# Joining the convolution-output stage and the relation-table stage of a graph network kernel

## The reference

```python
# layer 1, its end
agg = segment_sum(m, dst)                       # 6250 x 64
h = agg @ W_lin2.T + b_lin2
out = h @ W_message_to_node.T                   # 6250 x 256
x = _layernorm(x + out, axis=-1)
# layer 2
hW = einsum('nd,rde->rne', x, weight)           # 8 tables of 6250 x 256
msg = hW[edge_type, src]
m = segment_sum(msg, dst)
x = _layernorm(x + (x @ sl_w.T + sl_b + m / deg), axis=-1)
```

## Time and profile before

| what | value |
|---|---|
| runs, median (lowest to highest) | 8941.31 us (8940.38 to 8955.18) |
| profiled execution, its time | 8943.65 us |
| profiled execution, its span | 8942.0 us |
| mean granted clock of TensorE | 0.747 of 2.4 GHz |
| first instruction of the convolution-output stage | 5191.19 us |
| first bias product of the relation stage | 5388.93 us |
| start of the last copy of the relation stage | 5869.93 us |

### The profile page before, as it was taken

One profiled execution on the slowest core, in us unless ns is written; L12 is line 12 of the kernel. 1 busy time (PEld: TensorE's weight loads), 2 busy tenths in 40 slices (PEclk: granted clock), 3 DMA queues, 4 the chain that ended last, 5 costly groups with the idle time before them and its releaser, 6 DMA issues. The chain is left out here.

```text
span 8942.0 us, 114148 instructions
## 1 busy us (share of the span) xinstructions
PE 6288.6 (70%) x23568; PEld 4316.3 (48%) x23569; DVE 4789.7 (54%) x9732; ACT 1926.0 (22%) x6808; POOL 4599.6 (51%) x4186
## 2 busy tenths in 40 slices
PE   4548899967789999676777778955555666666650
PEld 2236666635566666355666644434444443443330
DVE  4337766666566767675444431134444644444438
ACT  0223333312333333121000011100000222222221
POOL 0036666610466666004777710047777288888880
PEclk7668887777888878675555559977777788888885
DMA  1384444311444434122111123333333366666665
GB/s 38 106 216 112 112 111 111 107 46 56 149 110 112 110 108 115 36 66 62 31 31 30 31 61 133 135 107 104 104 104 104 79 68 68 68 68 68 68 68 175
DMA packets 578153, 801.90 MB, mean 90 GB/s; under 512 B 100092, under 2 KB 453709, under 8 KB 576718
## 3 DMA queue, kind: packets, MB, share of 16 engines
q0 software_dynamic: 269760, 484.09, 27.2%
q1 hardware_dynamic: 281230, 290.19, 10.8%
q10 hardware_dynamic: 27092, 26.85, 1.2%
HBM read 545.48 MB, written 255.28 MB: 90 GB/s over the span
## 5 line engine op out<-in xcount | busy, mean ns | idle before, releaser
L609 POOL DMA_INDIRECT at_x<-table,at_idx x1664 | 1626.2, 977 | 1976.2 <-ACT at_idx L726 1009.1
L2279 POOL DMA_INDIRECT acc<-sc_rows,sc_idx x832 | 1353.3, 1627 | 298.4 <-DMA acc<-sc_rows,sc_idx 185.0
L684 PE MATMUL at_psO<-at_x,at_main 128*128 128x273 f32 x3328 | 1136.7, 471 | 244.9 <-DVE agg L875 240.2
L1679 POOL DMA_INDIRECT rel_x<-rel_table,rel_idx x832 | 793.0, 953 | 963.2 <-DVE rel_sums L1760 710.0
L1679 POOL DMA_INDIRECT conv_x<-conv_table,conv_idx x832 | 808.4, 972 | 767.0 <-DVE conv_msg L1763 513.7
L684 PEld LDWEIGHTS at_psO<-at_x,at_main 128*128 128x128 f32 x3328 | 709.0, 225 | 536.3 <-issue 378.6
L1732 PE MATMUL rel_psO<-rel_x,rel_hot 128*128 128x256 f32 x1664 | 607.6, 544 | 466.6 <-DMA rel_x<-rel_table,rel_idx 394.5
L2319 PE MATMUL sc_psR<-gated,sc_pick 128*128 x1664 | 593.9, 454 | 455.0 <-ACTq L2357 451.2
L875 DVE TENSOR_TENSOR agg<-agg,at_psO 128x273 f32 x1664 | 725.4, 436 | 246.1 <-DVE agg L875 166.5
L1732 PEld LDWEIGHTS rel_psO<-rel_x,rel_hot 128*128 128x128 f32 x1664 | 463.5, 285 | 611.1 <-issue 471.6
L765 ACT COPY at_row<-at_psO 1x273 f32<-1x273 f32 x1664 | 543.0, 374 | 599.7 <-PE at_psO L684 593.5
(11 more groups left out here) (412 smaller groups left out, 9192.8 us busy)
## 6 DMA issues: line engine op xcount, KB each, us to landing
at_place<-places SPq DMA_DIRECT2D x208, 256.0 KB
rel_table<-rt_rows SPq DMA_DIRECT2D x50, 1024.0 KB
at_x<-table,at_idx POOLq DMA_INDIRECT x1664
acc<-zeros ACTq DMA_DIRECT2D x4, 6553.5 KB, 63.1
la_t<-acc SPq DMA_DIRECT2D x40, 642.5 KB
conv_attr<-in_attr_T SPq DMA_DIRECT2D x832, 6.0 KB
conv_x<-conv_table,conv_idx POOLq DMA_INDIRECT x832
rel_x<-rel_table,rel_idx POOLq DMA_INDIRECT x832, 2.8
```

Of the source, the lines that this page charges most:

```text
L609: pool.indirect_dma_start(x[b][:, j, 0:TABW], None, d.table[0:NR, :], bass.IndirectOffsetOnAxis(ap=idx[b][:, j:j + 1], axis=0)).then_inc(x ...
L684: ins = nc.tensor.matmul(psO[j % BANKS][:, 0:AGG], main[b % 2][:, j, :], x[b][:, j, 0:AGG], start=True, stop=True)
L1679: pool.indirect_dma_start(x[b][:, j, 0:WIDE], None, table, bass.IndirectOffsetOnAxis(ap=idx[b][:, j:j + 1], axis=0)).then_inc(x_ready[b], 16)
L2279: pool.indirect_dma_start(d.acc[k][0:NR + P, :], bass.IndirectOffsetOnAxis(ap=idx[b][:, j:j + 1], axis=0), rows[b % 2][:, j, :], None, com ...
```

## The change

Both phases become one, `phase_conv_rel`. The output tiles of chunk 0 are made in a prologue. After that each chunk of relation tiles carries the five output tiles of the next chunk between its products: two in its first relation tile, one each in the second, third and fourth (`CONV_AT`), none in the fifth. The chunk's norm follows on VectorE after the fourth tile, its square root on ScalarE comes inside the fifth tile. The normalized chunk `y` stays in SBUF: it is not stored to `h2` and not loaded again, and transposes and residual sums read it there. The transposes of tile n+1 stand inside tile n, between pairs 1 and 2; those of a chunk's first tile stand at the end of the chunk before, behind a wait for `y_done`. The turned sums and the output product have one PSUM bank each (`psCT`, `psCO`) where they had two; with `psT`, `psB` and the four `psO` that makes eight. The weights of the relations are loaded at the start of the joint phase, behind the first two loads of `x`. Cut to its core:

```diff
-def phase_conv_out(nc, m, d, sem):
...
-def phase_rel_tables(nc, m, d, w, sem):
...
+def phase_conv_rel(nc, m, d, w, sem):
...
+    CONV_AT = {0: (0, 1), 1: (2,), 2: (3,), 3: (4,)}
...
+        psCT = ps("psCT", [FILT, P])
+        psCO = ps("psCO", [P, D])
+        psT = ps("psT", [P, 2, P])
+        psB = ps("psB", [P, D])
+        psO = [ps(f"psO{q}", [P, 2, D]) for q in range(PAIRS)]
...
+                for b in range(2):
+                    sp.dma_start(x[b][:], chunk_of(d.h, b)).then_inc(x_in[b], 16)
...
+                def chunk(c, b, turn):
+                    if not (isinstance(c, int) and c >= NCK - 2):
+                        sp.wait_ge(y_done, c + 1)
+                        sp.dma_start(x[b][:], chunk_of(d.h, c + 2)).then_inc(x_in[b], 16)
+                    for t in range(CT):
+                        n = c * CT + t
+                        q = parity(b, t)
+                        sp.wait_ge(base_done, n + 1)
+                        sp.dma_start(tile_of(d.base, n), base[q][:]).then_inc(base_stored[q], 16)
+                        for e in range(2):
+                            sp.wait_ge(o_copied[e], n * 2 + 4)
+                        sp.dma_start(d.rel_table.rearrange("(r n) k -> n r k", r=N_REL)[bass.ds(n * P, P), :, :], rows[q][:]).then_inc(stored[q], 16)
+                chunks(sp, chunk)
...
+                def conv_turn(n, q):
+                    pe.wait_ge(a_ready, n + 1)
+                    if not (isinstance(n, int) and n == 0):
+                        pe.wait_ge(ct_copied, n)
+                    nc.tensor.matmul(psCT[:], a[q][:], m.ident[:], start=True, stop=True).then_inc(ct_ready, 1)
+                def conv_out(n, q):
+                    pe.wait_ge(ct_copied, n + 1)
+                    if not (isinstance(n, int) and n == 0):
+                        pe.wait_ge(taken, n)
+                    nc.tensor.matmul(psCO[:], m.ones[0:1, :], m.b_conv_out[:], start=True, stop=False)
+                    nc.tensor.matmul(psCO[:], aT[q][:], m.w_conv_out[:], start=False, stop=True).then_inc(co_ready, 1)
+                def turn(n, yb, t):
+                    if not (isinstance(n, int) and n == 0):
+                        pe.wait_ge(t_copied, n)
+                    for k in range(2):
+                        ins = nc.tensor.transpose(psT[:, k, :], y[yb][:, t, k * P:(k + 1) * P], m.ident[:])
+                    ins.then_inc(t_ready, 1)
+                def pair(n, q, r):
+                    pe.wait_ge(o_copied[r % 2], n * 2 + r // 2 + 1)
+                    for k in range(2):
+                        ins = nc.tensor.matmul(psO[r][:].rearrange("p a n -> p (a n)"), hT[q][:, k, :],
+                                               wr[:, k, 2 * r:2 * r + 2, :].rearrange("p a n -> p (a n)"), start=(k == 0), stop=(k == 1))
+                    ins.then_inc(o_ready, 1)
+                for n in range(CT):
+                    conv_turn(n, n % 2)
+                    conv_out(n, n % 2)
+                pe.wait_ge(w_ready, 4 * 16)
+                pe.wait_ge(y_done, 1)
+                turn(0, 0, 0)
+                def chunk(c, b, it):
+                    for t in range(CT):
+                        n = c * CT + t
+                        q = parity(b, t)
+                        conv = CONV_AT.get(t, ()) if more(c) else ()
+                        pe.wait_ge(t_copied, n + 1)
+                        pe.wait_ge(base_done, n)
+                        nc.tensor.matmul(psB[:], m.ones[0:1, :], bs[:], start=True, stop=False)
+                        for k in range(2):
+                            ins = nc.tensor.matmul(psB[:], hT[q][:, k, :], ws[:, k, :], start=False, stop=(k == 1))
+                        ins.then_inc(base_ready, 1)
+                        pair(n, q, 0)
+                        if conv:
+                            conv_turn((c + 1) * CT + conv[0], parity(1 - b, conv[0]))
+                        pair(n, q, 1)
+                        if conv:
+                            conv_out((c + 1) * CT + conv[0], parity(1 - b, conv[0]))
+                        if t < CT - 1:
+                            turn(n + 1, b, t + 1)
+                        pair(n, q, 2)
+                        if len(conv) > 1:
+                            conv_turn((c + 1) * CT + conv[1], parity(1 - b, conv[1]))
+                        pair(n, q, 3)
+                        if len(conv) > 1:
+                            conv_out((c + 1) * CT + conv[1], parity(1 - b, conv[1]))
+                        if t == CT - 1 and more(c):
+                            pe.wait_ge(y_done, c + 2)
+                            turn(n + 1, 1 - b, 0)
+                chunks(pe, chunk)
...
+                def conv_a(n, q):
+                    if not (isinstance(n, int) and n < 2):
+                        act.wait_ge(ct_ready, n - 1)
+                    nc.scalar.copy(a[q][:], m.sums[:, bass.ds(n * (FILT + 1), FILT)]).then_inc(a_ready, 1)
+                def conv_t(n, q):
+                    act.wait_ge(ct_ready, n + 1)
+                    if not (isinstance(n, int) and n < 2):
+                        act.wait_ge(co_ready, n - 1)
+                    nc.scalar.copy(aT[q][:], psCT[:]).then_inc(ct_copied, 1)
+                def root(c):
+                    act.wait_ge(eps_ready, c + 1)
+                    nc.scalar.activation(sd[:, 1, :], sd[:, 0, :], ACT.Sqrt).then_inc(sd_ready, 1)
+                def turned(n, q):
+                    act.wait_ge(t_ready, n + 1)
+                    if not (isinstance(n, int) and n < 2):
+                        act.wait_ge(o_ready, (n - 1) * PAIRS)
+                    nc.scalar.copy(hT[q][:], psT[:]).then_inc(t_copied, 1)
+                def copy_pair(n, q, r):
+                    act.wait_ge(o_ready, n * PAIRS + r + 1)
+                    nc.scalar.copy(rows[q][:, 2 * r:2 * r + 2, :], psO[r][:]).then_inc(o_copied[1], 1)
+                conv_a(0, 0)
+                for n in range(CT):
+                    conv_a(n + 1, (n + 1) % 2)
+                    conv_t(n, n % 2)
+                root(0)
+                turned(0, 0)
+                def chunk(c, b, it):
+                    for t in range(CT):
+                        n = c * CT + t
+                        q = parity(b, t)
+                        conv = CONV_AT.get(t, ()) if more(c) else ()
+                        def side(k):
+                            tt = conv[k]
+                            nn = (c + 1) * CT + tt
+                            qq = parity(1 - b, tt)
+                            conv_t(nn, qq)
+                            if not (isinstance(nn, int) and nn == NT - 1):
+                                conv_a(nn + 1, 1 - qq)
+                        if conv:
+                            side(0)
+                        act.wait_ge(stored[q], use_of(b, t, it) * 16 + 16)
+                        copy_pair(n, q, 1)
+                        if t < CT - 1:
+                            turned(n + 1, 1 - q)
+                        if len(conv) > 1:
+                            side(1)
+                        if t == CT - 1 and more(c):
+                            root(c + 1)
+                        copy_pair(n, q, 3)
+                        if t == CT - 1 and more(c):
+                            turned(n + 1, 1 - q)
+                chunks(act, chunk)
...
+                def conv_add(n, yb, t, turn):
+                    if t == 0:
+                        dve.wait_ge(x_in[yb], turn * 16 + 16)
+                    dve.wait_ge(co_ready, n + 1)
+                    v.tensor_tensor(y[yb][:, t, :], psCO[:], x[yb][:, t, :], ALU.add).then_inc(taken, 1)
+                def norm(c, yb):
+                    ch.turn(c)
+                    dve.wait_ge(taken, c * CT + CT)
+                    norm_chunk(v, dve, ch, y[yb], st, mv, sd, eps_ready, sd_ready, y_done, held, c)
+                    ch.close()
+                for t in range(CT):
+                    conv_add(t, 0, t, 0)
+                norm(0, 0)
+                dve.wait_ge(y_done, 1)
+                def chunk(c, b, it):
+                    for t in range(CT):
+                        n = c * CT + t
+                        q = parity(b, t)
+                        conv = CONV_AT.get(t, ()) if more(c) else ()
+                        turn1 = it if b == 0 else it + 1
+                        dve.wait_ge(base_ready, n + 1)
+                        dve.wait_ge(base_stored[q], use_of(b, t, it) * 16 + 16)
+                        v.tensor_tensor(base[q][:], psB[:], y[b][:, t, :], ALU.add).then_inc(base_done, 1)
+                        dve.wait_ge(stored[q], use_of(b, t, it) * 16 + 16)
+                        dve.wait_ge(o_ready, n * PAIRS + 1)
+                        nc.vector.tensor_copy(rows[q][:, 0:2, :], psO[0][:]).then_inc(o_copied[0], 1)
+                        if conv:
+                            conv_add((c + 1) * CT + conv[0], 1 - b, conv[0], turn1)
+                        dve.wait_ge(o_ready, n * PAIRS + 3)
```

(11 more changed lines are left out.)

273 lines of the change are left out of this document (72 added, 201 removed).

## The result

The changed kernel took 8803.95 us, the median of 4 runs (8777.18 to 8858.18), and the kernel before 8940.84 us beside it: ratio 0.9855 with a 95% interval of 0.9805 to 0.9904. A second series gave 8799.64 (5 runs) against 8924.59 (21 runs), ratio 0.9856 (0.9835 to 0.9877). The forecast was 8821, between 8796 and 8852, and faster.

A forecast was written before the change was run, and what follows sets the result against it. TensorE was taken to bound both stages, through low clock and waits between products. Terms 24.2 + 451.1 + 76.5 + 3.4 + 2 + 1 = 558 us replace 678.7, 121 less: 8821 us, between 8804 and 8842 (wider range 8796 to 8852).

The forecast's parts named there:

- prologue to the first bias: Chunk 0's five output tiles and norm, nothing overlapping, up to the first relation bias: 24.2 us.
- 50 relation tiles: Joint loop: 40 tiles at 8.91 us, 9 chunk-end tiles at 9.57, the last at 8.6; sum 451.1 us.
- 45 output tiles: Output tiles inside relation tiles at the high clock: 1.7 us each, 76.5 us in all (48 to 131).
- start at the low clock: The loop begins at the low clock, as before: its first tile takes 3.4 us more than a steady one.
- norm late at chunk ends: Allowance of 2 us for TensorE waiting on the norm at some of nine chunk ends.
- semaphores behind the stage: Clearing of semaphores, formerly between the stages, now stands behind both: 1 us.
- Bound: Both stages go by TensorE; losses are the output stage's 1.2 GHz clock and the waits between products.
- Relation tile: Tile without output tile falls from 9.57 to 8.91 us, its transposes made inside the tile before.
- rival 2: Interleaving costs more: output tiles 2.3 us, or the root late at nine chunk ends; 8845 to 8870 us; 15%.
- The norm: At a chunk's end `y_done` comes 8.0 to 8.2 us into the fifth tile, with 0.3 us to spare.
- Rival 1: Weight loads in the dense stream all hide: 40 us more gain, 8781 us, half of it 8801; 10%.
- Rival 3: Joint loop loses the high clock and the kernel gets slower: 9073 us with half of it low; 4%.

The follow-up runs named there:

- experiment 2: Changed kernel with each tile's transposes back at that tile's own start: stage 597.4 us, 38.2 more than 559.2; ratio to the kernel before 0.9918.
- experiment 6: Changed kernel with both kinds of bias products made with 128 rows of weights in place of one: stage 535.3 us, 24 less.
- experiment 7: Changed kernel with the root ahead of pair 1's copy and the next chunk's first transposes between pairs 2 and 3: stage 552.7 us, 6.5 less.
- experiment 8: Changed kernel without bias products on TensorE (65th row of output weights, relation bias added by VectorE): stage 472.7 us, ratio to the kernel before 0.9757.
- experiment 3: Changed kernel with output tiles and norm between the chunks, nothing beside them: stage 679.2 us, 120 more; ratio to the kernel before 1.0005.
- experiment 5: Changed kernel with the next chunk's square root moved behind ScalarE's copy of pair 3: stage 603.8 us, 44.6 more.
- experiment 1: Changed kernel once more, no edit: stage 559.2 us, the rest of the span 8262.8 us (8215.5 in the first profile).
- experiment 4: Kernel before the change with unused full products added behind its output tiles: output stage 206 us (182 before), ratio 1.0027.

## Why the prediction was right

It was right in direction and mechanism, and the sum came within 3 us of the stage. That closeness is in part luck: the output tiles took 10.6 us more than predicted, and the relation tiles 5.5 and the chunk ends 2 less. The sum, term by term, against the profile after (measured terms are rounded and add up to 559.8):

| term | predicted | measured |
|---|---|---|
| prologue to the first bias | 24.2 | 24.1 |
| 50 relation tiles | 451.1 | 445.6 |
| 45 output tiles | 76.5 | 87.1 |
| start at the low clock | 3.4 | 3.0 |
| norm late at chunk ends | 2 | 0 |
| stage | 557 | 559.7 |
| semaphores behind the stage | 1 | 1.0 |

The last term is the way from the last copy to the next phase's first one: 6.33 us now (5698.55 to 5704.88), 5.36 before. A tile of the last chunk, which carries no output tile, by TensorE's bias and the next:

```profile
5663.57 0.69 PE L1982 MATMUL cr_psB<-cr_bs,ones 1*128 1x256 f32 x2
...
5672.35 0.69 PE L1982 MATMUL cr_psB<-cr_bs,ones 1*128 1x256 f32 x2
```

- **Bound.** TensorE's stream sets the stage, as argued: it is busy 526 of the loop's 533 us, and every change of that stream (experiments 2, 6, 7, 8) moved the stage by what the records say.
- **Relation tile.** 8.77 us without output tile (5663.57 to 5672.35), 8.91 predicted. Transposes cost 0.22 there, not 0.3, and the step into the bias 0.1, not 0.15. Chunk-end tiles stayed at 9.57.
- **Output tile, the mis-sized term.** 12.54 us for the tile with two (5437.55 to 5450.09) and 10.74 with one: less 8.77 each, five of them cost 9.68, so 1.94 each and not 1.70. Turn, bias and output take 0.37, 0.63, 0.62, which is the 1.6 of the prediction; but pair 0 takes 1.81 ahead of the turn and pair 1 1.91 ahead of the bias where 1.72 was even, and the transposes 0.28 behind the output. Of the 0.6 us that rival 2 put on top of 1.70 for steps on both sides, 0.24 came. Experiment 6 shows what the steps are and takes 0.16 of them away.
- **The norm.** `y_done` came at 7.9 us into the fifth tile (8.0 to 8.2), the cover was 0.6 to the product and 0.2 to its weight load (0.3). Nothing was paid.
- **Rival 1**, all weight loads pulled ahead, was wrong for this kernel: 0.63 for a one-row bias in a dense stream, with records on either side. The sentence of the Trainium skill ("TensorE: Matmul & The Clock Gate", section "Step-by-step: what each phase is for"), by which a load is pulled ahead when row groups don't conflict or the background buffer is the target, agrees with the traces for some forms and not for all: with 65 or 128 rows and 128 columns of weights the load began 0.43 us ahead of its product, with 1 or 64 rows, or with 64 columns, it began with the product, and so did the load of a full product right behind one of these (experiments 6 and 8). Which of the two conditions of the page fails there, no run shows.
- **Rival 3**, the clock, did not come, but it was less far off than its 4% said. Experiments 2, 3 and 5 bring the low clock back: with a wait of 0.46 us behind a run of small products (in three chunks of nine), in output tiles with nothing beside them, and with a wait of 2.8 us.
- **The median.** 8821 was 17 and 21 us high against the two series. The stage doesn't explain it, since it took 3 us more than predicted and not less; the part ahead does, by the scatter of experiment 1, which is in the kernel before as well (8941 in the first series, 8925 in the second). So the median is a weaker confirmation than the stage.
- **A slip without effect.** The prologue's "3.5 MB" is 3.7 in the decimal megabytes of the earlier trace rows. Nothing waited for them: the first transposes waited for `y`.

## What to carry to other kernels

Two stages that one engine bounds, one with dense large products and one with small sparse ones, are worth joining tile by tile: here the interleaving alone made the difference between 0.9856 and 1.0005, since it hid the small stage's waits (65 us in experiment 3) and ran its products at the high clock. Judge such a change by the stage's length in profiles, not by the whole time, where untouched stages scatter by 50 us. And look at the number of rows of the products in the dense stream: a bias as a one-row product cost more than its columns, and leaving the two kinds out, with the 64-row product widened to 65, took 86 us off the stage.

## What the runs showed that was not expected

- A product with 1 or 64 rows of weights beside products with 128 costs about 0.2 us more than its columns at 2.4 GHz, and 0.1 us on its neighbour; with 65 rows it costs nothing extra (0.62 against 0.44 us for the same 256 columns). The records put it on the weight load, which begins with the product and not 0.43 us ahead of it; a turn with 128 rows and 64 columns of weights shows the same.
- The clock falls while TensorE is busy: 191 of 195 us busy at a granted clock of 0.57 in experiment 4.
- A wait of 2.8 us costs about 5.0 (experiment 5: 44.6 us by nine), because the clock goes with it.
- The part ahead of the stage, the same code before and after the change, ran 52 us shorter in the first profile than in that of the kernel before, all of it ahead of 4131 us. Why stays open.
